# Attention: which probability tiles TensorE sums and which GpSimd adds, with ScalarE's output cast placed four head steps later

## The reference

```python
dots = jnp.einsum('bhid,bhjd->bhij', q, k) * scale
dots = jnp.where(causal_mask, -jnp.inf, dots)
attn = jax.nn.softmax(dots, axis=-1)
out = jnp.einsum('bhij,bhjd->bhid', attn, v)
```

## Time and profile before

| | us |
|---|---|
| median of the runs | 2617.73 |
| the profiled execution, its own time | 2619.38 |
| its span in the trace | 2617.6 |
| TensorE busy in the span | 2421.4 (93%) |
| VectorE busy | 1718.9 (66%) |
| GpSimd busy | 1118.5 (43%) |
| ScalarE busy | 1102.5 (42%) |

### The profile page before, as it was taken

One profiled execution on the slowest core, in us unless ns is written; L12 is line 12 of the kernel. 1 busy time (PEld: TensorE's weight loads), 2 busy tenths in 40 slices (PEclk: granted clock), 3 DMA queues, 4 the chain that ended last, 5 costly groups with the idle time before them and its releaser, 6 DMA issues. The chain is left out here.

```text
span 2617.6 us, 36273 instructions
## 1 busy us (share of the span) xinstructions
PE 2421.4 (93%) x13556; PEld 1013.8 (39%) x13556; DVE 1718.9 (66%) x3957; ACT 1102.5 (42%) x2066; POOL 1118.5 (43%) x404
## 2 busy tenths in 40 slices
PE   7999799999999999989946799999999999999998
PEld 3444223333323232323214354454445444454543
DVE  5433687777767677767405577767677776767665
ACT  4331156666666666666623242332324232322320
POOL 0000379989898989898952111102111211101100
PEclk9999799999999999999977899999999999999999
DMA  7864312212121213040021101010100101010000
GB/s 254 298 206 156 92 38 54 58 42 58 42 63 37 71 33 86 14 118 16 24 104 50 45 1 62 1 46 17 40 22 1 62 1 46 17 46 17 1 17 17
DMA packets 130443, 155.00 MB, mean 59 GB/s; under 512 B 19838, under 2 KB 98174, under 8 KB 129245
## 3 DMA queue, kind: packets, MB, share of 16 engines
q1 hardware_dynamic: 130269, 152.69, 19.1%
HBM read 99.96 MB, written 52.17 MB: 58 GB/s over the span
## 5 line engine op out<-in xcount | busy, mean ns | idle before, releaser
L762 ACT ACTIVATE probs<-st_ps 128x512 f32<-128x512 f32 (+3 forms) x1280 | 610.2, 535 | 339.9 <-PE st_ps L865 194.4
L637 POOL TENSOR_TENSOR total<-total,probs 128x2048 f32<-128x2048 f32 (+3 forms) x200 | 706.2, 3531 | 77.2 <-ACT probs L762 58.6
L804 DVE TENSOR_REDUCE seg_max<-s_ps 128x1 f32<-128x512 f32 x768 | 505.9, 685 | 139.2 <-PE s_ps L851 137.0
L865 PE MATMUL st_ps<-q_pair,k_pair 98*128 98x512 f16 (+3 forms) x1280 | 445.2, 362 | 34.9 <-ACT probs L762 28.8
L851 PE MATMUL s_ps<-k_pair,q_pair 96*128 96x512 f16 (+3 forms) x1280 | 446.1, 364 | 33.1 <-DVE seg_max L804 11.6
L1429 PE MATMUL fps<-x2T,w_p_hi 128*128 128x512 f16 x1024 | 317.3, 379 | 0.0
L885 PE MATMUL o_ps<-probs,v_sb 128*32 128x512 f32 (+3 forms) x2560 | 307.2, 553 | 0.0
L808 DVE CUSTOM_DVE_ANT_0 s_ps<-s_ps,later 128x384 f32<-128x384 f32 (+3 forms) x512 | 250.7, 497 | 85.8 <-issue 82.4
L1429 PE MATMUL fps<-w_p_hi,hT 128*128 128x512 f16 x1024 | 305.9, 380 | 0.0
L865 PEld LDWEIGHTS st_ps<-q_pair,k_pair 98*128 98x128 f16 x1280 | 125.0, 99 | 345.3 <-ACT probs L762 244.8
L1133 POOL TENSOR_TENSOR rstd<-rstd,keep_power 128x4 f32<-128x4 f32 x24 | 26.0, 1085 | 542.0 <-DVE rstd L1254 542.0
(11 more groups left out here) (164 smaller groups left out, 3403.5 us busy)
## 6 DMA issues: line engine op xcount, KB each, us to landing
k_pair<-k_parts SPq DMA_DIRECT2D x96, 128.0 KB, 3.9
q_pair<-q_parts SPq DMA_DIRECT2D x96, 128.0 KB, 4.9
x_raw<-xT_in SPq DMA_DIRECT2D x8, 1024.0 KB, 6.1
q_parts<-qk_out SPq DMA_DIRECT2D x32, 256.0 KB, 3.7
k_parts<-qk_out SPq DMA_DIRECT2D x32, 256.0 KB, 3.8
piece_raw<-w_in SPq DMA_DIRECT2D x8, 1024.0 KB, 8.7
v_rows<-v_out SPq DMA_DIRECT2D x32, 256.0 KB, 2.1
w_parts<-piece_cut SPq DMA_DIRECT2D x8, 1024.0 KB, 5.6
```

The lines of the kernel that those rows point to most:

```text
L637: last = nc.gpsimd.tensor_tensor(summed[:, :, off:], other[:, :, off:], probs[:, k % NP, :, off:], ALU.add)
L762: nc.scalar.activation(probs[:, k % NP, h, off:], st_ps[:, p % (2 * NVU) % RING, off:], ACT.Exp, scale=SCALE).then_inc(exp_done.sem, 1)
L804: nc.vector.reduce_max(highest, s_ps[:, slot], AX.X).then_inc(s_read.sem, 1)
L865: last = nc.tensor.matmul(st_ps[:, slot, off:], k_pair[a][:, h, kt * P:(kt + 1) * P], q_pair[a][:, c, h, off:], start=True, stop=not diagonal)
```

## The change

Four edits go together.

- `SUMMED` names the tiles that TensorE sums. Of the first chunk these are now all four (before: none, GpSimd added them), with their true widths. Of the second and third chunk they stay as they were (kt 2; kt 2 and 5). Of the fourth they are kt 3, 7 and 11 (before: 2, 5, 8 and 11).
- The first chunk has no totals any more. Its sums stand 12, 10, 8 and 6 head steps after their tiles (`FIRST_SUMS`), and ScalarE's copy of `o_ps` waits for a count of its own (`first_ready`), its copy of `den_ps` for the last of these sums.
- The two buffers of `total` alternate over three chunks a group (`total_of`).
- `UPPER` is SCALED + 12 where it was SCALED + 8; `LOWER`, `STORED` and `TAIL` hang on it and move by four head steps as well.

```diff
-    POOLED = [[n for n, (k, kt) in enumerate(KU) if k == c and (kt >= c * TT or kt % 3 != 2)]
-              for c in range(CPB)]
+    SUMMED = [(0, 1, 2, 3), (2,), (2, 5), (3, 7, 11)]
+    POOLED = [[n for n, (k, kt) in enumerate(KU) if k == c and kt not in SUMMED[c]] for c in range(CPB)]
+    TOTALLED = CPB - 1
...
+    FIRST_SUMS = 12, 10, 8, 6
...
-    UPPER = SCALED + 8
+    UPPER = SCALED + 12
...
+    def total_of(c):
+
+        return c // CPB * TOTALLED + c % CPB - 1
...
-                    summed = total[:, c % 2]
+                    t = total_of(k // NKU * CPB + c)
+                    summed = total[:, t % 2]
...
-                        pool.wait_ge(den_ready.sem, den_ready.at(i, k // NKU * CPB + c - 2))
+                        pool.wait_ge(den_ready.sem, den_ready.at(i, t - 2))
...
                 c = chunk_at(s, TAKEN[0], first, end)
                 if c is not None:
-                    act.wait_ge(pv_done.sem, pv_done.at(i, c // CPB * NKU + LAST_TILE[c % CPB]))
+                    if c % CPB == 0:
+                        act.wait_ge(first_ready.sem, first_ready.at(i, c // CPB))
+                    else:
+                        act.wait_ge(pv_done.sem, pv_done.at(i, c // CPB * NKU + LAST_TILE[c % CPB]))
...
-                    act.wait_ge(den_ready.sem, den_ready.at(i, c))
+                    if c % CPB == 0:
+                        act.wait_ge(pv_done.sem, pv_done.at(i, c // CPB * NKU + LAST_TILE[0]))
+                    else:
+                        act.wait_ge(den_ready.sem, den_ready.at(i, total_of(c)))
...
                 if k % NKU in POOLED[c]:
                     last.then_inc(pv_done.sem, 1)
+                elif final:
+                    last.then_inc(first_ready.sem, 1)
...
-                opens = all(n in POOLED[c] for n, (x, _) in enumerate(KU) if x == c and n < k % NKU)
+                opens, closes = kt == SUMMED[c][0], k % NKU == LAST_TILE[c]
+                off = max(kt - c * TT, 0) * P
                 if opens:
                     pe.wait_ge(den_taken.sem, den_taken.at(i, k // NKU * CPB + c - 1))
                 for h, out in enumerate(heads):
-                    last = nc.tensor.matmul(den_ps[out, :], ones[:], probs[:, k % NP, h], start=opens, stop=False)
+                    last = nc.tensor.matmul(den_ps[out, off:], ones[:], probs[:, k % NP, h, off:], start=opens,
+                                            stop=closes)
...
+                for kt, lag in enumerate(FIRST_SUMS):
+                    k = tile_at(s, lag, first, end)
+                    if k is not None and KU[k % NKU] == (0, kt):
+                        sums(i, k)
                 k = tile_at(s, SUMS, first, end)
-                if k is not None:
+                if k is not None and KU[k % NKU][0] > 0:
                     sums(i, k)
                 c = chunk_at(s, TOTALS, first, end)
-                if c is not None:
+                if c is not None and c % CPB > 0:
                     totals(i, c)
```

More of the change, by code:

```diff
@@ L580, in self_attention @@
         pv_done = Count(nc, stack, "pv_done", 2 * NKU)
-        den_ready = Count(nc, stack, "den_ready", 2 * CPB)
+        den_ready = Count(nc, stack, "den_ready", 2 * TOTALLED)
+        first_ready = Count(nc, stack, "first_ready", 2)
         o_taken = Count(nc, stack, "o_taken", 2 * CPB)
@@ L830, in _ @@
         def _(pe):
-            for count in (st_ready, pv_done, den_ready, s_ready):
+            for count in (st_ready, pv_done, den_ready, first_ready, s_ready):
                 count.lead(pe)
@@ L898, in sums @@
                 for h, out in enumerate(heads):
-                    last = nc.tensor.matmul(den_ps[out, :], ones[:], probs[:, k % NP, h], start=opens, stop=False)
+                    last = nc.tensor.matmul(den_ps[out, off:], ones[:], probs[:, k % NP, h, off:], start=opens,
+                                            stop=closes)
                 last.then_inc(pv_done.sem, 1)
             def totals(i, c):
-                opens = all(n in POOLED[c % CPB] for n, (x, _) in enumerate(KU) if x == c % CPB)
-                if opens:
-                    pe.wait_ge(den_taken.sem, den_taken.at(i, c - 1))
+                t = total_of(c)
                 pe.wait_ge(added.sem, added.at(i, adds_upto(c // CPB * NKU + LAST_TILE[c % CPB]) - 1))
                 for h, out in enumerate(heads):
-                    last = nc.tensor.matmul(den_ps[out, :], ones[:], total[:, c % 2, h], start=opens, stop=True)
+                    last = nc.tensor.matmul(den_ps[out, :], ones[:], total[:, t % 2, h], start=False, stop=True)
                 last.then_inc(den_ready.sem, 1)
```

## The result

The changed kernel has a median of 2633.55 us over 5 runs (2629.61 to 2635.37) against 2617.73 of the kernel before (2616.26 to 2622.35, 5 runs): a ratio of 1.0057, 95% interval 1.0043 to 1.0071. It is slower by 0.6%, inside the stated range of 2609 to 2642, and 13.5 us above the time that was forecast. Its profiled execution took 2631.46 us with a span of 2629.7.

A forecast was written before the change was run, and what follows sets the result against it. GpSimd's chain of 109.85 us plus TensorE's 16.0 and 0.1 was to set a 126.0 us turn, 0.6 shorter. Middle turns -3, seventh -1, last +4.65, first +1.5: together +2, hence 2620 us (8 in 10: 2609 to 2642).

The forecast's parts named there:

- Who bounds, and where: GpSimd's chain from tile 7's exp to its last addition (109.85 us) plus TensorE's totals to next tile 7 (16.0) sets the turn.
- TensorE's sums: First chunk: four batches added, totals gone, +1.6 us a turn (bounds +1.15 and +2.0), wholly on the path.
- The wait comes back at the totals: Head step 11: the wait taken from the cast returns, 1.8 us before the product and 2.5 at the totals.
- The sum: Whole stage: turn of 126.0 us, 0.6 less a turn; all groups together +2 us, giving 2620.
- Main case: Turn of 126.0 us, clock lost at the totals in no or one turn: 2620 (2616 to 2623), chance 0.42.
- The clock at the totals: Waits before the totals might drop the clock, 1.6 to 5 us a turn; a fall at the cast stayed as likely.
- Rival 1: Clock falls at the new wait before the totals, 2.8 us a turn; 2640 in seven turns; chance 0.38 from two turns up.
- The DMAs moved with the cast: SyncE's store up to 6 us longer, six load DMAs ahead of the first lap: costed at nothing.
- The last group: No TensorE work to hide behind, so GpSimd's new fourth-chunk addition costs its full +4.65 us.
- the seventh turn: Seventh group, whose turn holds a DMA delay of its own: -1 us.
- the first: First group loses a 2.5 us pause but then runs into GpSimd's chain: about +1.5 us.
- The rule of the clock: Skill page blames mid-kernel clock loss on longer pauses; neither cast nor totals would cost clock, time 2620.

The follow-up runs named there:

- a3: Kernel before with only the fourth chunk's edit (TensorE sums tiles 3, 7 and 11 in place of 2, 5, 8 and 11): 2622.6 us, ratio 1.0012.
- b1: Kernel before with the later cast and the fourth chunk's tiles 3, 7 and 11 on TensorE, first chunk left to GpSimd: 2621.6 us, ratio 1.0008.
- b5: Changed kernel with 16 more products by zeros a group on TensorE, right ahead of the wait at the fourth chunk's totals: 2621.5 us, ratio 1.0007.
- a2: Kernel before with only the first chunk's sums moved to TensorE, cast and fourth chunk as before: 2632.1 us, ratio 1.0047.
- a4: Changed kernel with the fourth chunk's sums put back to tiles 2, 5, 8 and 11: 2596.2 us, ratio 0.9911.
- c2: Kernel before with the later cast, but SyncE's store kept at its old head step: 2617.5 us, ratio 0.9994.
- a1: Kernel before with only the cast four head steps later, the store moving with it: 2583.8 us, ratio 0.9861.
- d1: Kernel before with only SyncE's store four head steps later: 2615.8 us, ratio 0.998.
- c1: Kernel before with GpSimd's scaling four head steps earlier, cast unmoved, and SyncE's store four head steps later: 2584.6 us, ratio 0.987.
- b3: Kernel before with GpSimd's scaling four head steps earlier, cast and store unmoved: 2619.1 us, ratio 0.9996.

## Why the prediction came out as it did

*Who bounds, and where (right).* In the changed kernel the circle of GpSimd's chain and TensorE's first chunk sets the turn, as the sum had it; a3, b1 and b5 show the same, with totals 0.1 us behind GpSimd's end. The chain was put at 109.85 us and is 110.2 to 110.4; that the idle 4.19 us are filled by the new 4.65 is seen in the trace of after.

*TensorE's sums (right).* +1.6 us were worked out, a2 and a4 show 15.9 - 14.4 = 1.5. They lie wholly on the path, and GpSimd's relief is worth nothing, as a2 shows alone.

*The wait comes back at the totals (right).* 1.8 and 2.5 us were worked out ahead of head step 11's product and the totals; 1.39 and 2.28 us were measured in nearly every group. TensorE's lead is thus some 3.7 us, where 5.5 were worked out; the sum doesn't use it.

*The sum (right without the clock).* Main case 2620; b5, where the clock holds, has 2621.5.

*The clock at the totals (the wrong choice of the likelier case).* The main case needed the clock to hold in all turns or all but one. It fell in every turn, for 3.4 or 6.8 us. The step that failed is the guess that a fall at the cast was as likely and would take its place: the pause there, 1.2 to 2.2 us foreseen and 1.05 to 1.88 us measured in the second to seventh group, was followed by half clock in one of them only (782.2 to 785.6). Even there it did not take the other's place: the clock fell again at the next totals, at 840.3. Rival 1 had this at 2.8 us a turn; the lead-in shows 1.3 to 2.4 (17.2 to 18.3 against b5's 15.9), and b5 puts the whole at 12 us. That is most of the difference between 2620 and 2633.6.

*The DMAs moved with the cast (one wrong, one small).* "I cost these at nothing" was wrong twice. SyncE's store had been costed as a possible loss only, with the inverse's DMAs in view. Its move past the loads is what lets the later cast bring anything: c2 against a1 is 34 us. In the sum for the changed kernel the error stayed hidden, because the turn was worked out as if TensorE came early to the totals, which, by c2 and a1, takes the store's new place; the changed kernel with the old place was not run. And the six loads put ahead of the first lap do delay something: the first scores come 2.9 us later than before (305.68 against 302.80). Some 1.9 of these are the row DMA's longer way from issue to landing (5.9 us for 4.0); it was issued 1.0 us later as well, which the loads, issued behind it, don't explain. By tile 7 1.4 us are left.

*The last group* (+4.65 foreseen, +4.7 seen), *the seventh turn* (-1 foreseen, -1.0 seen) and *the first* (+1.5 foreseen; seen +1.4 before its tile 7 and +2.7 behind) are the other terms. That the seventh agrees is luck: without the clock's fall it would be -3.0 (b5: 126.5 against 129.5), since the store's new place took away the DMA delay of that group, as in d1. The stages behind, put at nothing, are 2.3 us shorter; why stays open.

The rule of the clock named in the prediction, from the Trainium skill's page "TensorE: Matmul & The Clock Gate", section "Why this matters for your kernels", would have left the clock alone at pauses of 1.39 and 2.28 us; the trace disagrees, with a granted clock of 0.50 at them.

## What to carry to other kernels

In a pipeline of several engines an edit is worth what it takes off the closed path that sets the period: work moved off an engine in a stretch where it idles anyway brings nothing, and work moved onto it in the stretch where it has no pause costs its full time, even if the engine's total falls. A stall can hide behind another; judge an edit that moves several queues at once by each queue alone (here the store's move was a by-product of the cast's, and without it the gain of 34 us was zero). Where an idle time is counted on as cover, ask whether the same change removes the stall that made it.

## What the runs showed of the hardware

A pause of TensorE of 2.28 us with another of 1.39 us ending 1.1 us ahead of it (in one turn without it) came with a granted clock of 0.50 for 3.4 or 6.8 us in all turns of the changed kernel. In the fifth turn the clock fell 0.5 us after the second pause had begun (966.6 against 966.10). With products by zeros in the second (b5, none longer than 1.5 us left there) it fell in no turn. More products, less time. Of c1's five pauses of 1.70 us at the totals one was met by half clock, at 769.5, and four were not.

The issue of the two row DMAs on SyncE took 6.10 and 5.80 us directly behind seven loads (b3, c2) and 1.15 us where SyncE had stood 6.5 us between the loads and the store (a1).
